# New order strings for a fused self-attention, cross-attention and two-layer decoder kernel

## The reference

```
self   S  16 heads of 8 features; scores y.y/sqrt(8), softmax, every head's
          weights applied to the whole x, one [2048,128] product; residual, layernorm
cross  C  query from the stream, key and value from ctx, 16 heads of 8, allowed
          where |i-j| <= 64; softmax, output product; residual, layernorm
local  twice (layers 0 and 1): half of the features shifted by one token, qkv
       product, 8 heads of 64, q and k normalised and rotated, allowed where
       j <= i and j >= i-64, softmax, output product, residual; then layernorm of
       the shifted stream, a gated GELU network of 341 hidden features, residual
       a last residual and layernorm after layer 1
```

## Time and profile before

| | |
|---|---|
| median of three runs | 1466.55 us |
| the profiled execution's own time | 1461.15 us |
| its span, first to last instruction | 1459.3 us |
| PE busy | 1333.5 us, 91% |
| DVE busy | 1026.3 us, 70% |
| ACT busy | 938.5 us, 64% |
| POOL busy | 885.3 us, 61% |
| mean granted TensorE clock | 0.965 |

### The profile page before, as it was taken

One profiled execution on the slowest core, in us unless ns is written; L12 is line 12 of the kernel. 1 busy time (PEld: TensorE's weight loads), 2 busy tenths in 40 slices (PEclk: granted clock), 3 DMA queues, 4 the chain that ended last, 5 costly groups with the idle time before them and its releaser, 6 DMA issues. The chain is left out here.

```text
span 1459.3 us, 39524 instructions
## 1 busy us (share of the span) xinstructions
PE 1333.5 (91%) x12472; PEld 928.8 (64%) x12472; DVE 1026.3 (70%) x2900; ACT 938.5 (64%) x2563; POOL 885.3 (61%) x1291
## 2 busy tenths in 40 slices
PE   5889999999999999999999999999999999998864
PEld 3556666666666666666666666666666666666543
DVE  2467776777777777777777777777777777776431
ACT  1256765677776667777766677776666777765552
POOL 2046666666666666666667666666666666666542
PEclk8799999999999999999999999999999999998785
DMA  5000000000000000000000000000000000000000
GB/s 158 10 5 4 5 7 7 5 4 5 4 4 5 5 5 5 4 4 4 5 5 5 5 5 4 4 4 5 5 5 5 4 5 3 5 5 3 3 3 4
DMA packets 22220, 12.55 MB, mean 9 GB/s; under 512 B 5878, under 2 KB 21024, under 8 KB 22176
## 3 DMA queue, kind: packets, MB, share of 16 engines
q1 hardware_dynamic: 21600, 10.96, 2.6%
q10 hardware_dynamic: 576, 1.05, 0.2%
HBM read 9.91 MB, written 2.10 MB: 8 GB/s over the span
## 5 line engine op out<-in xcount | busy, mean ns | idle before, releaser
L1212 POOL TENSOR_TENSOR local_e<-local_e,local_rd 128x512 f32<-128x512 f32 x128 | 133.0, 1039 | 238.2 <-DVE local_rd L1033 238.2
L848 ACT ACTIVATE local_e<-local_ps,local_bias,local_rn 128x128 f32<-128x128 f32 x512 | 230.8, 482 | 7.3 <-DVE local_bias L1029 7.3
L1191 POOL TENSOR_TENSOR local_rn<-local_sc,half_neg 128x8 f32<-128x8 f32 x128 | 211.3, 1658 | 14.4
L586 PE MATMUL self_ps<-self_z,self_e 128*128 128x129 f32 x1024 | 155.8, 291 | 2.6 <-ACT self_e L779 1.4
L1024 DVE TENSOR_REDUCE local_m<-local_ps 128x4 f32<-128x512 f32 x128 | 87.8, 686 | 96.4 <-PE local_ps L509 96.4
L586 PEld LDWEIGHTS self_ps<-self_z,self_e 128*128 128x128 f32 x1024 | 130.7, 196 | 13.8 <-issue 2.7
L955 DVE SCALAR_TENSOR_TENSOR self_y<-self_ps,self_rd,self_y 128x128 f32<-128x128 f32 x448 | 133.3, 345 | 8.8 <-issue 0.6
L606 PE MATMUL local_ps<-wz,self_kT 128*128 128x512 f32 x256 | 134.1, 627 | 1.1 <-ACT local_v L832 0.6
L848 ACT ACTIVATION_READ_ACCUMULATOR local_e<-local_ps,local_bias,local_rn 128x1 f32 x512 | 117.4, 229 | 0.0
L828 ACT ACTIVATE local_sq<-local_ps 128x512 f32<-128x512 f32 x128 | 76.1, 595 | 61.4 <-PE local_ps L665 58.4
L665 PE MATMUL local_ps<-wqkv_s,local_xT 128*128 128x512 f32 x128 | 71.4, 639 | 26.6 <-ACT local_xT L824 26.6
(11 more groups left out here) (172 smaller groups left out, 3392.6 us busy)
## 6 DMA issues: line engine op xcount, KB each, us to landing
self_xin<-x SPq DMA_DIRECT2D x32, 64.0 KB, 1.8
cross_cin<-ctx_in SPq DMA_DIRECT2D x32, 64.0 KB, 1.8
out<-local_out SPq DMA_DIRECT2D x32, 64.0 KB, 1.6
wqkv_s<-wqkv SPq DMA_DIRECT2D x2, 768.0 KB
wz<-w_heads ACTq DMA_DIRECT2D x4, 256.0 KB, 6.3
w_r<-w SPq DMA_DIRECT2D x2, 341.0 KB
con<-consts SPq DMA_DIRECT2D x1, 640.0 KB, 6.0
wo_s<-wo SPq DMA_DIRECT2D x2, 256.0 KB
```

The costliest lines, as they stand in the source:

```text
L586: last = nc.tensor.matmul(bank[:, 129 * j:129 * j + 129], s.e[:, h0 + j, :], s.z[:, h0 + j, :], start=True, stop=True)
L848: nc.scalar.activation(s.e[:, a, p, :], bank[:, 128 * p:128 * p + 128], ACT.Exp, bias=s.bias[:, a, p:p + 1], scale=s.rq[:, a, p:p + 1], ac ...
L1191: nc.gpsimd.tensor_tensor(s.rn[:, heads], s.sc[:, heads], half_neg[:, 0:LH], ALU.pow).then_inc(done, 8)
L1212: nc.gpsimd.tensor_tensor(s.e[:, a, :, :], s.e[:, a, :, :], s.rd[:, a, :].unsqueeze(2).to_broadcast([128, LH // 2, 128]), ALU.mult)\
```

## The change

The four strings are replaced by four others with the same letters. Two of them:

```diff
 ORDER_TENSOR = (
-    "OONAAONASPBPABPBCZSCBZSZZASACSBBDCSECSSCSDSDSDCSDEEMCCECME")
+    "ONOAAONASPBAPBZPSZBCSBCASZASCDZSCBBSCSECSDSDCDSSDEEMCCEMCE")
 ORDER_VECTOR = (
...
 ORDER_GPSIMD = (
-    "NANNSCBOBSSASAAAAABBBBBBAABDDEEPMMMSPSCC")
+    "NANNSBCSSBASAAAAAOABBABBBBBDDEEMMMSPSCCP")
```

More of the change, by code:

```diff
@@ L70 @@
 ORDER_TENSOR = (
-    "OONAAONASPBPABPBCZSCBZSZZASACSBBDCSECSSCSDSDSDCSDEEMCCECME")
+    "ONOAAONASPBAPBZPSZBCSBCASZASCDZSCBBSCSECSDSDCDSSDEEMCCEMCE")
 ORDER_VECTOR = (
-    "NNNONOAAAAPAPBBBBSSBCCSSCBACCODDCCDDESDSSEEDPESSSSSSEESSSDMSSMMCCMPCCSEC")
+    "NNNONOAAAAAAPBBSPSBSSBCCCBCDDCBPDCCSDDSESEDESSESSSEESSSDOSMMMCMCSSCCESCP")
 ORDER_SCALAR = (
-    "OAANSAPBABCBZBCZSZAZASBSBDSSDCDDEECCDDEEDCCEEEM")
+    "OAANSABPABZZBCBSCAZASSZDSSBBDCDDECCDEDEEDCCEEEM")
 ORDER_GPSIMD = (
-    "NANNSCBOBSSASAAAAABBBBBBAABDDEEPMMMSPSCC")
+    "NANNSBCSSBASAAAAAOABBABBBBBDDEEMMMSPSCCP")
 def shape_constants():
```

## The result

| | before | after |
|---|---|---|
| median | 1463.13 us (14 runs, 1459.95 to 1468.26) | 1468.70 us (14 runs, 1465.99 to 1477.56) |
| profiled execution, span | 1459.3 us | 1466.4 us |
| mean granted TensorE clock | 0.965 | 0.962 |
| start of the first L572 of the loop | 238.54 us | 234.76 us |
| the 25 passes from there to the last one | 1049.94 us | 1061.94 us |

The ratio is 1.0039 [1.0022, 1.0055]: slower by 5.6 us, under the 0.5% that I had set as the bound of no change, and 14.7 us over my 1454. The span grew by 7.1 us: 3.8 gained in the fill, 12.0 lost in the loop, 1.1 gained in the drain (169.7 us from the last L572 to the end, before 170.8).

The account below looks back on a forecast made before the run. PE was taken to set the pass, its waits being what can be won. Terms summed to -0.36 us per pass, -9.4 in 26: 1451.8 from 1461.15, plus 2.7 for run spread, 1454.5; 8-in-10 range 1446 to 1478.

Parts of the forecast that it names:

- What bounds the kernel: PE, full nearly everywhere, sets the 42.00 us pass; two thirds of its waits lie at the pass's end, a chain.
- the end of the pass: Chain from L645 to L662: L662 comes 0.07 us earlier per pass, bounds 0.2 earlier and 0.2 later.
- the 0.2 that L993 wins: On DVE at the pass's end, L993 could start about 0.2 us earlier, as a layernorm step ahead of it moved.
- Fill and drain: Stretches before and after the loop: taken as 0 change, bounds -4 and +4 us.
- wait -0.20: PE's wait ahead of L709 of layer 0 goes, covered by L529, L534 and L499: -0.20 us per pass.
- pause -0.09: PE's pause ahead of L665, between L672 and L665, goes as L744 stands between: -0.09 us per pass.
- shapes -0.15: Changes of tile shape on PE fall from 26 to 24 per pass, 0.1 to 0.2 each: -0.15 us per pass.
- new waits +0.15: New short waits at L672 of layer 0 and around the second self score: +0.15 us per pass, bounds 0 and +0.6.
- The first rival: POOL's L1203 starts before DVE's L1029 of layer 0 and holds it up: +0.49 us per pass, 1476.6 us; chance 0.27.
- The second rival: No change: tight places cost 0.1 each, new waits 0.5 not 0.15, -0.01 us per pass, 1463 us; chance 0.20.

Follow-up runs that it names:

- e11_root_late: The new order with only the first POOL step of layer 1's last norm (L1119) moved early, its root left late: 1452.74 us, 0.9912 of before.
- e6_before_delayed: The order of before with one more POOL sum of 0.45 us ahead of L1223 of layer 1, into an unread tile: 1501.01 us, 1.0243 of before.
- e1_fill: The new order with PE making two of layer 0's L744 products twice, in the idle time ahead of L662: 1454.27 us, 0.9947 of before.
- e14_fill_second: The new order with two unread 128x128 products on PE between L662 and L665 of layer 0: 1453.88 us, 0.9946 of before.
- e6b_before_delayed2: The order of before with two extra unread POOL sums ahead of L1223 of layer 1: 1527.26 us, 1.0428 of before.

## Why the prediction was wrong

**What bounds the kernel** held: PE sets the pass, the end of the pass is the chain, and no other engine became the bound. (More than the "two thirds" of its waits lie there: 1.66 of the 1.95 us that the prediction lists.)

**The step that failed is the end of the pass**, "I take -0.07, because both ends come from rows and the middle is near nothing". It measured +0.37, outside my bounds of -0.2 and +0.2. I set the 0.2 that L993 wins against part of the root. The win never reached the chain, as POOL still had local_ve and self_rs to do when cross_mv came (e11_root_late: 0.26), and the root ahead of the copy cost 0.28 by itself. I had priced each step on POOL's queue by its own wait and not laid them one behind the other from the moment that cross_mv is ready. In the rows, of the 0.37 are 0.11 there when DVE starts the cross output (4.19 behind L709, before 4.08), and 0.26 come between that and POOL's copy. The two parts that the experiments take away, 0.26 and 0.28, are more than 0.37 together, because the win of L993 then comes through. The prediction named this growth by more than 0.2 as what would make it wrong.

**What I hadn't priced at all is the clock.** I used it only to call the loop "1.00". In the earlier trace rows stood 0.62 and 0.81 of idle time side by side, and beyond them a step: with 0.12 more, in the new order, a third of the passes take 1.67 us more, and with 0.27 more in the order of before (e6_before_delayed) 18 of 25 hold a fall. That the waits bring the falls is shown from both sides (e1_fill, e14_fill_second; e6_before_delayed, e6b_before_delayed2).

On the profiled executions I had forecast -9.4 and 7.1 came, 16.5 apart. The 8 falls are 13.4 of that. A quiet pass won 0.06 and not 0.36, which is 7.5 in 25: 0.44 per pass too little at the end of the pass, 0.13 too much in the middle. Fill and drain give 4.9 back, and the rest, 0.5, is the 26th pass and rounding. So the mis-sized end cost twice: by itself, and by the falls that its longer wait brought. Without the falls the kernel is faster than before, 0.9947 of it in e1_fill.

**The middle** I had at -0.29 (wait -0.20, pause -0.09, shapes -0.15, new waits +0.15), and it measured -0.42. L709's wait went and L715 had none. The shapes I had too small, for another reason than their number: two pairs of blocks on different rows run at the same time, which saves 0.61. My "0.2 (into float32)" for a change had no row behind it; the earlier trace rows give 0.09 and 0.10. The new waits I had too small as well: L703 of layer 1 takes 0.15 more ahead of L727, L727 0.07 more, L556 of cross waits 0.17, and L672 of layer 0 had its pause of about 0.1. Two more tenths are no waits: L703 of layer 0 (0.09) and L750 of layer 1 (0.10) now stand directly ahead of a 32-row block, and pay what L606 paid there in the earlier trace rows. The sum came out near by two errors against each other; that is luck.

**The first rival** (L1029 held up by L1203) did not happen, because its condition did not: in every pass of the loop L1029 starts about 0.3 ahead of L1203. Whether L1203 would hold it up, these passes can't tell. Another step did:

```profile
376.63 1.26 POOL L1199 TENSOR_TENSOR local_cosp<-local_cosp,local_sinp 128x512 f32<-128x512 f32 x1
...
377.55 0.36 DVE L1029 TENSOR_TENSOR local_bias<-local_m,local_rn 128x4 f32<-128x4 f32 x1
...
377.86 1.04 POOL L1203 TENSOR_TENSOR local_cosp<-local_cosp,local_rn 128x512 f32<-128x512 f32 x1
```

L1029 takes 0.36, until L1199 ends, and not 0.16; over the passes of the loop it takes 0.35 to 0.43. POOL was later than I had placed it, so what stood in the way was L1199's last third of a us. In the drain one L1029 starts 0.22 into an L1199, and takes 1.06, until 0.02 behind its end:

```profile
1351.30 1.26 POOL L1199 TENSOR_TENSOR local_cosp<-local_cosp,local_sinp 128x512 f32<-128x512 f32 x1
```

```profile
1351.52 1.06 DVE L1029 TENSOR_TENSOR local_bias<-local_m,local_rn 128x4 f32<-128x4 f32 x1
```

So a 128x512 sum of POOL does hold L1029 up for as long as it still runs, as the earlier trace rows showed for L1212. This agrees with the Trainium skill, page "SBUF — State Buffer", section "SBUF: two separate sides". In the loop it costs little: the only wait on PE soon behind it that the order of before hasn't is 0.17 (0.22 in some passes) ahead of L556 of cross, where the rival's chain ends. No run takes it away by itself.

**The second rival**, no change, gave the nearest time, 1463, but by margins eaten with the pass at 42.0 everywhere, which isn't what happened. The time lies in my range of 1446 to 1478, but the range was that wide only for the first rival, so that is luck too. **Fill and drain** gained 4.9 us, a little outside my bounds of 4, and the fill alone varies by more than that between executions.

What stays open: why with waits of 0.74 and 0.81 in every pass just these 8 have a fall. They keep a pattern (pairs 85 us apart, 297 from pair to pair), and nothing in the two waits of the pass tells them apart.

## What to carry to other kernels

Read the idle times of TensorE that stand close together as one, and check in the trace whether the granted clock falls behind them in any pass: if it does in one, a tenth of a microsecond more may bring it in a third of them, as here. If a wait can't be removed, put matmuls into it. Where several engines' steps are moved to the end of a chain, lay out the slow engine's queue from the moment that its input is ready, and price what stands in it as a whole. A swap taken out of a found order can cost what it wins inside it, because its cover stays behind.

## What the runs showed of the hardware

- The granted clock fell to its lower level behind two short waits, 0.74 and 0.81 us, in a loop whose PE is busy for 95% of the time (1011.76 of 1061.94). The Trainium skill, page "TensorE: Matmul & The Clock Gate", section "HAM oscillation — how this bites in real kernels", tells of the clock falling behind one long wait for a DMA. No wait here is of that kind; the measurement decides, and here it was the two near waits together that counted. One fall costs 1.67 us in the new order; in e6_before_delayed the passes with one are 0.8 to 1.8 over those without.
- Two blocks of short matmuls on different 32-row groups of the array run in turns: 16 of them in 0.34 us where 8 take 0.33. The Trainium skill, page "TensorEngine Tiling (Array Packing)", section "Key Properties", says that a change of the tiling mode empties the engine and that tiles work in parallel. The trace agrees with the second; of the first it shows the price of going into a 32-row block and out of it, 0.09 and 0.10, but not what that time is spent on.
- A POOL sum of 128x512 holds up a DVE product with both inputs in SBUF until it ends: 0.16 undisturbed, 0.36 to 1.06 behind L1199, 0.39 behind L1212.
- Products that nobody needs, issued into one of two near waits, won 14.4 and 14.8 us (0.9% by the ratios to before) against the same kernel without them.
